# Routed experts' first layer: weights stationary, tokens moving, the expert's weights copied to a fixed place one slot ahead

## The reference, cut to what matters

```
x_red = x @ w_red;  logits = x_red @ wg_n.T;  gates = softmax(logits)
scores = max(gates);  idx = argmax(gates)
h = x @ W1[idx] + b1[idx]          # 256 -> 512
h = gelu(h)
o = (h @ W2[idx] + b2[idx]) * scores   # 512 -> 256
x = x + tanh(g_ffn[1]) * o
```

## Time and profile before

| what | value |
|---|---|
| median of 3 runs | 550.26 us (548.94 to 551.91) |
| the profiled execution, its own time | 554.43 us |
| its span, first to last instruction | 552.4 us |
| TensorE busy over the span | 444.7 us (80%) |
| VectorE busy | 342.7 us (62%) |
| ScalarE busy | 255.5 us (46%) |
| GpSimd busy | 116.7 us (21%) |
| mean granted clock of TensorE | 0.891 of 2.4 GHz |

### The profile page before, as it was taken

How to read it: one execution, slowest core, us unless ns; L and a number is a source line. 1 busy time by engine, 2 the same in 40 slices (tenths; PEclk the granted TensorE clock), 3 DMA queues, 4 the chain that set the end, 5 groups by cost and what they waited for, 6 DMA issues and landing times.

```text
span 552.4 us, 7862 instructions
## 1 busy us (share of the span) xinstructions
PE 444.7 (80%) x2372; PEld 295.6 (54%) x2373; DVE 342.7 (62%) x742; ACT 255.5 (46%) x461; POOL 116.7 (21%) x137
## 2 busy tenths in 40 slices
PE   2896869999995004999799999999976189999992
PEld 2585634444443003888466656666544047667672
DVE  0369795338997799643456676666766615555552
ACT  1234445559971894301465556556545034323310
POOL 4115224200000000400760000100011263543222
PEclk9976569999998555999799999999997579999998
DMA  7700000000001004000990000000006031212000
GB/s 239 202 2 1 1 1 2 0 0 0 0 18 32 0 0 93 1 1 1 358 400 4 0 1 2 1 1 1 1 16 215 16 100 39 68 48 53 26 26 1
DMA packets 27388, 27.19 MB, mean 49 GB/s; under 512 B 11579, under 2 KB 23554, under 8 KB 27107
## 3 DMA queue, kind: packets, MB, share of 16 engines
q1 hardware_dynamic: 25155, 21.73, 12.2%
q0 software_dynamic: 2208, 5.14, 3.2%
HBM read 22.63 MB, written 5.15 MB: 50 GB/s over the span
## 4 chain that ended last, share of the span: by engine, by line
PE 58%; DVE 14%; issue 8%; ACT 5%; DVEq 1%; POOL 1%; ACTq 0%; POOLq 0%
PE bank L1414 46%; PE bank L1644 5%; PE bank L1461 3%; PE bank L1788 2%; PE bank L1662 2%; DVE big_g L1112 2%; ACT tmp L827 1%; DVE amU L1124 1%; DVE amZ L1118 1%; DVE big_g L1166 1%; DVE mx L1258 1%; DVE big_g L1259 1%; DVE big_g L1255 1%; ACT big_u L728 1%; ACT tmp L824 1%
## 5 line engine op out<-in xcount | busy, mean ns | idle before, releaser
L1414 PE MATMUL bank<-yT,ffn_w 128*128 x192 | 85.2, 606 | 4.0 <-ACT yT L728 2.8
L1414 PEld LDWEIGHTS bank<-yT,ffn_w 128*128 128x128 f32 x192 | 37.2, 195 | 50.9 <-issue 49.7
L728 ACT ACTIVATE big_u<-bank 77x512 f32<-77x512 f32 (+3 forms) x102 | 57.7, 580 | 13.5 <-PE bank L1644 8.6
L1414 PE MATMUL bank<-ffn_w,big_u 128*128 128x256 f32 x192 | 44.0, 392 | 8.2 <-ACT big_u L728 8.2
L889 ACT ACTIVATE big_g<-big_g 128x308 f32<-128x308 f32 x64 | 29.4, 459 | 40.6 <-DVE big_g L1259 40.6
L1414 PE MATMUL bank<-k_blockdiag,big_g 128*128 128x308 f32 x128 | 45.7, 442 | 0.7 <-ACT yT L728 0.7
L1414 PEld LDWEIGHTS bank<-ffn_w,big_u 128*128 128x128 f32 x192 | 37.7, 198 | 13.7 <-ACT big_u L728 8.3
L1414 PE MATMUL bank<-big_g,yT 128*128 x92 | 44.1, 623 | 0.7 <-issue 0.7
L1414 PE MATMUL bank<-big_u,yT 128*128 x184 | 41.8, 380 | 1.6 <-DVE yT L1377 1.6
L1644 PE MATMUL bank<-ident,big_g 128*77 128x128 f32 x256 | 41.2, 285 | 0.8 <-ACT big_g L889 0.5
L728 ACT ACTIVATE yT<-bank 128x256 f32<-128x256 f32 (+1 forms) x47 | 17.3, 419 | 50.9 <-PE bank L1461 37.2
(11 more groups left out here) (265 smaller groups left out, 813.3 us busy)
## 6 DMA issues: line engine op xcount, KB each, us to landing
big_g<-in_L_ffn_W SPq DMA_DIRECT2D x1, 4096.0 KB, 14.5
big_u<-in_L_ffn_W SPq DMA_DIRECT2D x1, 4096.0 KB, 24.9
x_rows<-in_x SPq DMA_DIRECT2D x2, 1024.0 KB, 9.4
ffn_w<-in_L_ffn_b SPq DMA_DIRECT2D x1, 2048.0 KB, 25.9
tmp<-bias_by_distance SPq DMA_DIRECT2D x2, 616.0 KB, 5.6
token_rows<-x_rows SPq DMA_DIRECT2D x1, 1032.0 KB, 6.9
tmp<-in_L_ffn_b SPq DMA_DIRECT2D x1, 1024.0 KB, 5.3
token_rows<-x_rows SPq DMA_DIRECT2D x1, 774.0 KB, 9.6
```

Source lines behind the costliest of these rows:

```text
L728: act.activation(out_, in_, ACT.Copy, **k).then_inc(done, 1)
L1414: return pe.matmul(out_, lhsT=lhsT, rhs=rhs, start=first, stop=last)
```

## The change

`layer1` swaps its operands. The stationary operand is now a 128x128 piece of W1, the moving operand the 128 columns (tokens) of `ysT`. Eight matmuls per slot take the place of two: four pieces of the hidden values times two halves of the inputs. The result lies in PSUM as hidden values on partitions and tokens along the row, which is what `layer2` needs as its stationary operand. `hiddenT`, `hidden`, `hT` and their semaphores go.

W1 of a slot's expert is copied to a fixed place, `W1S` (two halves of 128 x 1024), before `layer1` reads it: for even slots by VectorE, for odd slots by ScalarE, each for the slot of the next pair. `layer1` waits for the copy instead of loading the expert's number. `B1` becomes 128 x 32, its hidden values on partitions, and `bias1` broadcasts it along the tokens. With one transpose less between the layers, `layer2` runs in the same step as `layer1`, and the steps shift by one.

```diff
@@ SyncE @@
-            sp.dma_start(B1, row(a["L1_ffn_b1"].rearrange("e h -> (e h)")).to_broadcast([P, E * HID])).then_inc(s.ld_b1, 16)
+            sp.dma_start(B1, a["L1_ffn_b1"].rearrange("e h -> (e h)").rearrange("(n p) -> p n", p=P),
+                         allow_slow_non_contiguous=True).then_inc(s.ld_b1, 16)
@@ ScalarE @@
+            def expert(i):
+                e = act.value_load(EXPS[0:1, 2 * i + 1:2 * i + 2], min_val=0, max_val=E - 1)
+                if i:
+                    act.wait_ge(s.h_ps, 2 * i)
+                act.activation(W1S[:, 1, :], W1f[:, ds(e * (CH * HID), CH * HID)], ACT.Copy).then_inc(s.w1_sb1, 1)
+            act.wait_ge(s.slots_sb, 1)
+            act.wait_ge(s.ld_w1, 16)
+            expert(0)
...
                 if len(now) > 1:
                     gelu(1, i)
+                if len(nxt) > 1:
+                    expert(i + 1)
                 for u in nxt2:
                     normalised(u, i + 2)
@@ VectorE @@
-                dve.tensor_tensor(hb[:, u, :], pb[2 + u], B1[:, ds(e * HID, HID)], ALU.add).then_inc(s.hb_sb, 1)
-            def hidden(u, i):
-                dve.wait_ge(s.hT_ps, 2 * i + u + 1)
-                dve.tensor_copy(hT[:, u, :], pb[4 + u]).then_inc(s.hT_sb, 1)
+                dve.tensor_tensor(hb[:, u, :].rearrange("p (j n) -> p j n", j=HJ),
+                                  pb[2 + u].rearrange("p (j n) -> p j n", j=HJ),
+                                  B1[:, ds(e * HJ, HJ)].unsqueeze(2).to_broadcast([P, HJ, P]), ALU.add).then_inc(s.hb_sb, 1)
+            def expert(i):
+                e = dve.value_load(EXPS[0:1, ds(2 * i, 1)], min_val=0, max_val=E - 1)
+                dve.tensor_copy(W1S[:, 0, :], W1f[:, ds(e * (CH * HID), CH * HID)]).then_inc(s.w1_sb0, 1)
...
                 for u in now:
                     bias1(u, i)
-                for u in prev:
-                    result(u, i - 1, first)
+                    if u == 0 and len(now) > 1:
+                        expert(i + 1)
                 for u in now:
-                    hidden(u, i)
+                    result(u, i, first)
@@ TensorE @@
             def layer1(u, i):
-                e = pe.value_load(EXPS[0:1, ds(2 * i + u, 1)], min_val=0, max_val=E - 1)
+                pe.wait_ge(s.w1_sb0 if u == 0 else s.w1_sb1, i + 1)
                 pe.wait_ge(s.ysT_sb, 2 * i + u + 1)
-                for ci in range(CH):
-                    ins = mm(pb[2 + u], ysT[:, u, ci * P:(ci + 1) * P], W1f[:, ds(e * (CH * HID) + ci * HID, HID)],
-                             ci == 0, ci == CH - 1)
+                for j in range(HJ):
+                    for ci in range(CH):
+                        ins = mm(pb[2 + u][:, j * P:(j + 1) * P], W1S[:, u, ci * HID + j * P:ci * HID + (j + 1) * P],
+                                 ysT[:, u, ci * P:(ci + 1) * P], ci == 0, ci == CH - 1)
                 ins.then_inc(s.h_ps, 1)
-            def hiddenT(u, i):
-                pe.wait_ge(s.gelu_sb, 2 * i + u + 1)
-                for j in range(HJ):
-                    ins = pe.transpose(pb[4 + u][:, j * P:(j + 1) * P], hb[:, u, j * P:(j + 1) * P], ident[:, :])
-                ins.then_inc(s.hT_ps, 1)
             def layer2(u, i):
...
                 pe.wait_ge(s.res_sb, 2 * i + u + 1)
-                pe.wait_ge(s.hT_sb, 2 * i + u + 1)
+                pe.wait_ge(s.gelu_sb, 2 * i + u + 1)
                 for j in range(HJ):
-                    ins = mm(pb[6 + u][:, 0:D], hT[:, u, j * P:(j + 1) * P], W2f[:, ds(e * (HJ * D) + j * D, D)],
+                    ins = mm(pb[6 + u][:, 0:D], hb[:, u, j * P:(j + 1) * P], W2f[:, ds(e * (HJ * D) + j * D, D)],
                              j == 0, j == HJ - 1)
-            def step(i, now, nxt, prev):
+            def step(i, now, nxt):
                 for u in now:
                     layer1(u, i)
                 for u in nxt:
                     inputs(u, i + 1)
-                for u in prev:
-                    layer2(u, i - 1)
                 for u in now:
-                    hiddenT(u, i)
+                    layer2(u, i)
```

More of the change, by code:

```diff
@@ L200, in __init__ @@
         self.gelu_sb = sem("gelu_sb")
-        self.hT_ps = sem("hT_ps")
-        self.hT_sb = sem("hT_sb")
+        self.w1_sb0 = sem("w1_sb0")
+        self.w1_sb1 = sem("w1_sb1")
         self.eo_ps = sem("eo_ps")
@@ L406, in flamingo_kernel @@
         W2 = part(BIGU, 0, [P, E * HJ, D])
-        B1 = part(FW, 0, [P, E * HID])
+        W1f = W1.rearrange("p n h -> p (n h)")
+        B1 = part(FW, 0, [P, E * HJ])
         B2 = part(TMP, 0, [P, E * D])
@@ L447, in flamingo_kernel @@
         hb = part(YW, 1024, [P, 2, HID])
-        hT = part(YW, 2048, [P, 2, HID])
+        W1S = part(FW, 512, [P, 2, CH * HID])
         res = part(YW, 3072, [P, 2, D])
@@ L1387, in result, with step @@
                                          ALU.mult, ALU.add).then_inc(s.res_sb, 1)
-            def step(i, now, prev, first=False):
+            def step(i, now, first=False):
                 for u in now:
                     bias1(u, i)
-                for u in prev:
-                    result(u, i - 1, first)
+                    if u == 0 and len(now) > 1:
+                        expert(i + 1)
                 for u in now:
-                    hidden(u, i)
+                    result(u, i, first)
             dve.sem_inc(s.res_sb, 2)
-            step(0, (0, 1), ())
+            dve.wait_ge(s.ld_w1, 16)
+            expert(0)
             c.enter(0, 2)
-            step(1, (0, 1), (0, 1), True)
+            step(0, (0, 1), True)
             c.leave(1)
[L1402 to L1408, removed]
+            with dve.Fori(1, NP) as i:
+                c.enter(i - 1, 2)
+                step(i, (0, 1))
+            c.leave(NP - 1)
+            c.enter(0, 1)
+            step(NP, (0,))
             c.leave(1)
@@ L1768, in _ @@
             pe.wait_ge(s.ld_w2, 16)
-            W1f = W1.rearrange("p n h -> p (n h)")
             W2f = W2.rearrange("p n h -> p (n h)")
@@ L1805, in step @@
                     inputs(u, i + 1)
-                for u in prev:
-                    layer2(u, i - 1)
                 for u in now:
-                    hiddenT(u, i)
+                    layer2(u, i)
             for u in range(2):
                 inputs(u, 0)
[L1812 to L1817, removed]
+            with pe.Fori(0, NP - 1) as i:
+                step(i, (0, 1), (0, 1))
+            step(NP - 1, (0, 1), (0,))
+            step(NP, (0,), ())
 _INS = ["x", "ctx_1024", "mask_BxS2_bf0", "g_xattn", "g_ffn",
```

## The result

The changed kernel took 556.62 us (median of 4 runs, 555.91 to 559.42) where the kernel before took 549.6 (4 runs, 548.25 to 551.91): ratio 1.0121, interval 1.008 to 1.0163, so 1.2% slower. The forecast was 539.7. The profiled execution took 556.37 us, its span 554.5.

A forecast was written before the change was run, and what follows sets the result against it. Only TensorE's own work was taken to bound the expert stage. Terms -10.0 + 0.9 - 1.1 - 0.45 = -10.6 us took the median from 550.26 to 539.7 us, with an 8-in-10 range of 537.0 to 545.5.

The forecast's parts named there:

- Is another engine late in 7.42 us?: Expert stage, TensorE's new cycle per pair: no other engine late, tightest spare 0.4 to 0.6 us at `layer2(1)`.
- the new road between the layers is late: Rival: `layer2(1)` waits for `gelu(1)`; at 0.4 us a pair, 4.4 us in all, kernel at 544.1; 14 in 100.
- Start -1.1: Start of the expert stage: waits at the first odd gelu and the loop's entry go, -1.1 us.
- The "0.68" that "go": The wait of 0.68 us for the first odd gelu, said to vanish in the new order.
- Transposes removed, -10.0: Expert stage: `hiddenT`'s 92 transposes at 0.109 us each leave TensorE's path, -10.0 us.
- `layer1` turned round: Expert stage: 16 passes of 128 columns a slot at 0.110 us each, 40.5 us against 39.6, +0.9 us.
- Weight loads set the pace: Rival: every `layer1` pass waits for its load, up to 0.191 us a pass, kernel at 569.4; 7 in 100.
- Copies: W1 copies in each pair: 0.75 us on VectorE, 1.05 on ScalarE, covered by `layer2` and costing nothing.
- End: Last single slot: 1.55 us between `layer1` and `layer2` where TensorE waited 2.0 us before, -0.45 us.
- B1: Load of B1 as 4096 single elements, lying under the attention: nothing either way.

The follow-up runs named there:

- s1: The changed kernel unaltered, run again in a group without late signals: 540.82 us, ratio 0.9807.
- e1: The changed kernel with both copies of W1 on ScalarE and none on VectorE: 552.65 us, ratio 1.0045.
- t1: The changed kernel with eight gathers ahead and a GpSimd instruction of about 1.05 us between a pair's two scatter-and-gather couples: 540.99 us, ratio 0.9821.
- e2: The changed kernel with `layer2` of a pair a step later, behind the next pair's `layer1`, and an own buffer for the gelu's output: 544.77 us, ratio 0.9885.
- r3: The changed kernel with `layer2` a step later and twelve gathers ahead, the same kernel as e2, repeated: 546.13 us, ratio 0.9901.
- e7: The kernel before with only `layer1` cut into passes of 128 columns, tokens still stationary, transposes kept: 552.43 us, ratio 1.0049.
- e3: The kernel before with both copies of W1 added, written to a place nobody reads: 550.06 us, ratio 0.9981.
- r2: The changed kernel with eight gathers ahead in place of twelve, in a group with late signals: 551.61 us, ratio 1.002.
- e4: The changed kernel with all 23 gathers issued in one burst before the first scatter, in place of 12: 561.87 us, ratio 1.0195.
- t2: The changed kernel unaltered, run again beside t1 in a group without late signals: 541.09 us, ratio 0.9808.
- s3: The changed kernel with a GpSimd instruction of 1.05 us after every second indirect transfer: 551.87 us, ratio 0.9992.
- e8: The changed kernel with the 11 gathers in the pairs replaced by plain loads by SyncE, of rows not those wanted: 538.63 us, ratio 0.9798.
- s2: The changed kernel with the in-pair gathers as plain loads by SyncE, e8 once more: 539.56 us, ratio 0.9776.
- r1: The changed kernel unaltered, repeated in a group with late signals: 556.12 us, ratio 1.0108.
- groups 1 and 3: The sets of runs e1 to e4 and r1 to r4, each on one chip; the kernel before took 551.08 and 550.82 us there.
- r4: The kernel before with eight gathers ahead in place of twelve: 577.98 us, ratio 1.0515.

## Why the prediction was wrong

The changed kernel has two times, and the kernel before one: unaltered, the changed kernel took 556.62 and 556.12 us where signals were late, 540.82 and 541.09 where none was; the kernel before 549.6 to 551.61 in all groups. The forecast of 539.7 describes the second case and gave the first no place.

- **The step that failed** is "Is another engine late in 7.42 us?", in its first assumption: "From TensorE's last pass to VectorE's start I use 0.15 us". That was read from one pair at 502 us. Where signals are late this hand-over took 1.7 to 5.5 us in five of the first six pairs (446.59 to 452.05 in the first). The step's own place was right: `layer2(1)` waiting for `gelu(1)`. But the 0.4 to 0.6 us that it found to spare there, and the 0.7 us at `gelu(0)`, do not exist even without a late signal: the hand-over to `bias1` is then 0.45 us from the third pair on (s1), since VectorE comes from `result(1)` and has to read the expert's number first, for which the step had no term. So a late signal costs nearly all of its lateness: in pair 3 the hand-over took 1.79 us, 1.35 more than in a quiet pair, and the first pass of `layer2(1)` came 1.29 us later (1.13 of it shows as idle time).
- The rival "the new road between the layers is late" names that place, but at 0.4 us a pair and through slower work of the engines. Through VectorE's copy it came true even where no signal is late, at 0.13 us a pair (7.60 against e1's 7.47). The late signals on the same road are another mechanism, and 10 us of stalls.
- **Start -1.1** failed with it: the first pair stood 4.99 us and ran at half clock behind it (granted clock 0.50 from 453.74 to 457.30 us). Sum of the loss: from the first transposes to TensorE's last pass the changed kernel took 107.5 us in the first profile and 91.7 in s1, 15.8 more. Stalls are 10.25 of it. Lower clock is most of the rest: the first `layer1` took 5.85 us against 4.40 (granted clock 0.57 against 0.82; this one is not the late signals' doing, since t1, with nothing late, took 5.81 at 0.59), the `layer2(1)` behind the stall 3.57 against 1.73, the next `layer1` 4.50 against 3.57, together 4.2.
- The kernel before hides the same lateness: there `layer2` runs a step later. Its own late signal in the first pair was to be seen in the profile before, and the prediction passed it over:

```profile
455.27 0.69 DVE L1377 COPY yT<-bank 128x512 f32<-128x512 f32 x1 [3.38 <-remote]
```

  TensorE's record of the work behind it (`hiddenT`) ended at 452.49, 2.8 us earlier. The "0.68" that "go" belonged to this first pair too. The change moved `layer2` into the same step and left next to nothing of the spare that a whole step had given; e2 gives the step back and, with the stall at the start still there, has 544.77 us (546.13 as r3) in the late groups.
- **Transposes removed, -10.0**: right. The page's L1788 is gone.
- **`layer1` turned round**: right but for 0.6 us. By the starts of its passes it costs 0.1116 us a pass in all pairs at full clock, in the first profile, s1, e1 and e7 alike, and not 0.110; 368 x 0.0016 = 0.6 us. The cycle's other 0.13 us lies in `layer2`, by the road above.
- **Weight loads set the pace** (rival, and the estimate from the Trainium skill, "TensorE: Matmul & The Clock Gate", section "Back-to-back issue gap", of 0.156 us a pass and 556.4 us): the time came out within 0.3 us of it by accident, for another reason. With 0.1116 us a pass, 1.04 times streaming, the page's 1.45 is not seen here.
- **Copies**: 0.69 us on VectorE (forecast 0.75), 1.06 on ScalarE (1.05). Both are free in the kernel before (e3). In the changed kernel "the copies cost nothing" fails for VectorE's: it is a link of the road and costs the 0.13 us, about 1.2 us over nine pairs.
- **End**: 1.73 us between the last `layer1` and its `layer2` in place of 1.55, so -0.27 and not -0.45. **B1**: it landed in 22.6 us, and nobody waited for it.
- The 540.8 us of the groups without late signals lie 1.1 us above the forecast, but not because each term held: the cycle is 7.60 and not 7.42, 2 us over eleven pairs, and other differences made up for a part of it.

Shown by runs: the lateness comes by group and not by kernel; it costs the changed kernel 15 us and the kernel before nothing that can be measured; a step more between the layers absorbs it except at the start (e2, r3); a shorter first burst takes the first stall away (r2); VectorE's copy of W1 is what makes the quiet cycle 7.60 and not 7.47 (e1). Only argued: that GpSimd's indirect transfers, back to back, hold the signals. For it speaks that the lateness begins only with these transfers, that of the 44 waits on VectorE and ScalarE that end on "remote" (nine traces) 35 end 0.1 to 2.0 us behind the last transfer of a run, and that none comes after the last gather but one of e4's, 3.5 us behind it. The other eight, in e2, e4 and r3, end while a run is under way, so a run need not be over for a signal to pass. Against it stands that s1 and t2 do the same transfers with no effect. The runs meant to settle it, s3 and t1, fell into groups without late signals, and so did e8 and s2, which were to tell GpSimd's instructions from the rows' landing. Open too is what makes a group late. r1 and t2 carry the same chip number, so that number alone doesn't decide. One more sign goes with it without a gap: in the traces of the first measurement and groups 1 and 3 many semaphore updates have no record (of the 193 updates of the semaphore that counts the even slots' scattered rows, the first profile of the changed kernel holds 96, that of the kernel before 102, r1 96, r2 80, r4 119), in those of the other groups all 193 have. So the two kinds of group may differ in how they were recorded. Every run here was recorded, so whether an unrecorded execution would show the lateness is open as well.

## What to carry to other kernels

A road through several engines that by a sum has half a microsecond to spare may have none; price it by the worst hand-over in the trace, above all by waits that end on "remote", and not by one quiet pair, and count what an engine's sequencer does between two instructions. Follow each engine's order round once: here `result`, `bias1`, the copy and `bias1` closed a loop as long as the cycle, which neither the sum of busy times (about 4 us of 7.4) nor the chain of waits shows. Moving a consumer into the step of its producer spends the spare that covered such delays; keeping it a step later cost nothing here (541.5 against 541.9 us) and saved 10 us where signals were late (546.13 against 556.12, one group). A kernel that was measured once, on one chip, has one of its times.

The turned `layer1` with `layer2` a step later beat the kernel before in every group in which it ran: 544.77 and 546.13 us (twelve ahead, late groups), 541.5 (eight ahead and semaphores by pair, without late signals). It met the changed kernel itself only in group 3. Where no signal is late it is no faster than that (540.82 and 541.09).

## What the hardware showed that was not expected

- TensorE's semaphore updates, on different semaphores and for different readers, can come up to 5.3 us (6.0 in r3) after the work's record ends, in order and within 0.2 us of each other (451.92 to 452.10 in the first profile), in some groups of runs and never in others. A trace shows it as a wait that ends on "remote".
- The same kernel then has two times 2.8% apart (556.1 and 541.0 us), each with a scatter of under 1%, while another kernel beside it has one.
- In e4's burst of 29 us TensorE stood 9.88 us, and single passes of `layer1` had gaps of 0.44 and 1.13 us before them.
- 128 columns in float32 against 128-column weight loads cost 0.1116 us a pass at full clock, 4% over streaming.
- Between the end of `result(1)` and the start of `bias1(0)` VectorE's sequencer takes 0.78 us (502.80 to 503.58 in s1) to read one expert's number into a register, while VectorE does nothing.
